# One square instruction per context batch, and one scale per partition

## The reference, cut to what matters

```
x = x + tanh(g_xattn) * ( gelu(layernorm(x) @ ctx.T) @ ctx )      # per batch: 224x512 @ 512x750, 224x750 @ 750x512
x = x + tanh(g_ffn) * moe(layernorm(x))                           # gate, top 2 of 8, silu(x w1) * (x w3), w2
```

## Time and profile before

| | us |
|---|---|
| median of 3 runs | 688.33 (687.57 to 690.29) |
| the profiled execution's own time | 688.32 |
| its span, first to last instruction | 686.6 |
| first GELU of batch 1 to first GELU of batch 14 (13 steps) | 280.93 |
| PE / ACT / DVE / POOL busy, share of the span | 93% / 67% / 61% / 58% |
| mean granted clock of TensorE | 0.991 |

### The profile page before, as it was taken

One profiled execution on the slowest core, in us unless ns is written; L12 is line 12 of the kernel. 1 busy time (PEld: TensorE's weight loads), 2 busy tenths in 40 slices (PEclk: granted clock), 3 DMA queues, 4 the chain that ended last, 5 costly groups with the idle time before them and its releaser, 6 DMA issues.

```text
span 686.6 us, 15832 instructions
## 1 busy us (share of the span) xinstructions
PE 636.1 (93%) x4638; PEld 442.9 (65%) x4639; DVE 416.9 (61%) x1287; ACT 460.6 (67%) x771; POOL 395.6 (58%) x459
## 2 busy tenths in 40 slices
PE   2789999999999999999998999999999999999990
PEld 1677788788887888878885555455554554555550
DVE  3368788898889888898886644543333333333330
ACT  5899999899998999999974444444443444434440
POOL 4332347765666656776566777875555555565551
PEclk9999999999999999999999999999999999999996
DMA  7455558646686567666424565766666656666653
GB/s 216 128 171 157 160 150 200 182 143 181 163 171 195 160 154 189 174 170 179 119 83 120 93 132 93 121 102 120 111 108 121 117 100 122 111 108 118 118 102 55
DMA packets 51380, 94.77 MB, mean 138 GB/s; under 512 B 17024, under 2 KB 25344, under 8 KB 51312
## 3 DMA queue, kind: packets, MB, share of 16 engines
q1 hardware_dynamic: 34096, 60.02, 32.9%
q0 software_dynamic: 16400, 33.89, 27.6%
q10 hardware_dynamic: 816, 0.02, 0.1%
HBM read 61.89 MB, written 32.01 MB: 137 GB/s over the span
## 4 chain that ended last, share of the span: by engine, by line
DMA 26%; PE 11%; issue 5%; DVE 3%; POOL 3%; ACT 1%; POOLq 1%; SPq 0%; DVEq 0%; ACTq 0%
DMA out_rows<-ctx_raw,meta 23%; PE bank L1368 5%; DMA ctx_raw<-xf_rows,meta 3%; PE bank L1377 3%; POOL out_rows L537 2%; PE bank L1323 1%; POOLq L533 1%; PE bank L1357 1%; ACT ctx_raw L766 1%; DMA meta<-route_table 0%; PE bank L1257 0%; PE bank L1222 0%; POOL ctx_raw L525 0%; DVE ctx_part L825 0%; DVE ctxT L1155 0%
## 5 line engine op out<-in xcount | busy, mean ns | idle before, releaser
L1368 PE MATMUL bank<-w,ctxT 128*128 x756 | 173.4, 379 | 0.9 <-issue 0.9
L537 POOL DMA_INDIRECT out_rows<-ctx_raw,meta x63 | 100.3, 1593 | 99.4 <-DMA out_rows<-ctx_raw,meta 87.8
L1222 PE MATMUL bank<-ctx_part,a_part 125*112 125x512 f16 x576 | 135.1, 380 | 0.8 <-DVE a_part L834 0.8
L1368 PEld LDWEIGHTS bank<-w,ctxT 128*128 128x128 f16 x756 | 74.0, 98 | 75.9 <-issue 1.0
L1210 PE MATMUL bank<-xnT,ctxT 128*125 128x224 f16 x1152 | 118.2, 262 | 0.3 <-ACT ctxT L629 0.3
L1210 PEld LDWEIGHTS bank<-xnT,ctxT 128*125 128x125 f16 x1152 | 112.4, 139 | 0.4 <-issue 0.4
L777 ACT ACTIVATE ctxT<-bank,cols 128x256 f32<-128x256 f32 x63 | 29.9, 474 | 115.4 <-issue 84.8
L1222 PEld LDWEIGHTS bank<-ctx_part,a_part 125*112 125x112 f16 x576 | 71.4, 130 | 39.6 <-DVE a_part L834 0.8
L629 ACT ACTIVATE ctxT<-bank 128x1000 f16<-128x1000 f16 x96 | 94.5, 1005 | 3.0 <-PE bank L1177 3.0
L1377 PE MATMUL bank<-w2s,ctxT 128*128 x378 | 91.9, 379 | 1.5 <-DVE ctxT L1137 1.5
L489 POOL DMA_INDIRECT route_table<-route,pos_i x64 | 72.8, 1138 | 19.2 <-issue 17.2
(11 more groups left out here) (155 smaller groups left out, 987.5 us busy)
## 6 DMA issues: line engine op xcount, KB each, us to landing
ctx_raw<-in_ctx SPq DMA_DIRECT2D x48, 448.0 KB
w_raw<-in_L_ffn_w SPq DMA_DIRECT2D x24, 512.0 KB, 6.3
x<-in_x SPq DMA_DIRECT2D x16, 448.0 KB, 6.5
out_rows<-x SPq DMA_DIRECT2D x16, 448.0 KB
xf_rows<-xf SPq DMA_DIRECT2D x16, 448.0 KB, 4.4
ctx_raw<-in_ctx SPq DMA_DIRECT2D x48, 52.0 KB
meta<-route_table SPq DMA_DIRECT2D x66, 1.0 KB, 2.0
ctx_raw<-xf_rows,meta POOLq DMA_INDIRECT x66, 4.2
```

The lines of the kernel that those rows point to most:

```text
L537: g.indirect_dma_start(out=out, out_offset=bass.IndirectOffsetOnAxis(ap=meta[n][:, 0:1], axis=0), in_=y_sb[n % 2], in_offset=None, compute ...
L1222: ins = t_.matmul(O_ps[t][0:TT, :], a_part[ha][:, c, t * TT:(t + 1) * TT], ctx_part[u][hc][:, c, :], start=c == 0 and (ha, hc) == PARTS[0] ...
L1368: ins = t_.matmul(H_ps[u][:, :], rows, w, start=m == 0, stop=m == KD * len(PARTS) - 1)
```

## The change

The sums of squares of a context are now made by one instruction over all three thirds, 125 x 3072, instead of three of 125 x 1024 (`row_squares`, with the instruction at L611 of the new file). It waits for all three loads. Its unwanted output goes to rows 0 to 2 of both the high and the low part of the buffer, which are now two halves of one tensor. There is one sum and one scale for a partition; `scale_from` writes it three times, so that the readers of the scales stay as they are. The high parts of thirds 1 and 2 are made by one instruction of 125 x 2048 (`ctx_high_rest`), in the place where third 1's stood. The maximum over the thirds' totals is left out from batch 2 on. Batches 0 and 1 are begun as before.

```diff
-        ctx_part = [[sb(f"ctx_part{u}{h}", [CR, NC, D], F16) for h in range(2)] for u in range(2)]
+        ctx_both = [sb(f"ctx_part{u}", [CR, 2, NC, D], F16) for u in range(2)]
+        ctx_part = [[b[:, h, :, :] for h in range(2)] for b in ctx_both]
...
+                if copies > 1:
+                    exp = exp.to_broadcast([P, copies])
...
-                scale_from(ctx_sum[:, :], ctx_inv[u][:, :], ctx_s[u][:, :], 0, NQ).then_inc(ctx_scaled, NQ)
+                scale_from(ctx_sum[:, 0:1], ctx_inv[u][:, :], ctx_s[u][:, :], 0, 1, NQ).then_inc(ctx_scaled, NQ)
...
-                seq.done(g.tensor_scalar(ctx_max[:, :], ctx_gsum[:, 0:1], ctx_gsum[:, 1:2], ctx_gsum[:, 2:3], ALU.max, ALU.max))
-                seq.hold()
-                scale_from(ctx_max[:, :], all_inv[:, :], all_s[:, :], A_BITS).then_inc(all_scaled, 1)
+                gmax = ctx_gsum[:, 0:1]
+                if not later(i, 2):
+                    gmax = ctx_max[:, :]
+                    seq.done(g.tensor_scalar(gmax, ctx_gsum[:, 0:1], ctx_gsum[:, 1:2], ctx_gsum[:, 2:3], ALU.max, ALU.max))
+                    seq.hold()
+                scale_from(gmax, all_inv[:, :], all_s[:, :], A_BITS).then_inc(all_scaled, 1)
...
+            def row_squares(i, u):
+
+                for q in range(NQ):
+                    act.wait_ge(ctx_loaded[q], i * 32 + 32)
+                act.wait_ge(ctx_sum_ready, i * NQ)
+                act.wait_ge(ctx_scaled, i * NQ)
+                act.wait_ge(ctx_tot_made, i)
+                act.wait_ge(attn_part, (i - 2) * NQ + 2)
+                a.activation(ctx_both[u][:, :, 0:NC // 2, :], ctx_raw[0:CR, :, :].rearrange("p (h c) d -> p h c d", h=2), ACT.Square,
+                             accum_out=ctx_sum[0:CR, 0:1]).then_inc(ctx_sum_ready, NQ)
...
+            def ctx_high_rest(i, u):
+
+                act.wait_ge(ctx_scaled, i * NQ + NQ)
+                a.activation(ctx_part[u][0][:, 2:NC, :], ctx_raw[0:CR, 2:NC, :], ACT.Copy, scale=ctx_s[u][0:CR, 0:1].bitcast(F32)).then_inc(ctx_high, NQ - 1)
...
                     ctx_high_part(i + 1, w, 0)
-                    ctx_high_part(i + 1, w, 1)
+                    ctx_high_rest(i + 1, w)
                     ctx_tot_out(i + 1)
                     gelu(i, u, 1)
                 split_end(weight_tot_out, i, u, h)
-                ctx_high_part(i + 1, w, 2)
+                if not later(i, 1):
+                    ctx_high_part(1, 1, 2)
...
                 if two:
-                    ctx_squares(i + 2, 0)
-                    ctx_squares(i + 2, 1)
+                    row_squares(i + 2, u)
                 ctxT_out(i + 1, w, 4)
-                if two:
-                    ctx_squares(i + 2, 2)
                 ctxT_out(i + 1, w, 5)
```

More of the change, by code:

```diff
@@ L434, in inv_std, with scale_from @@
                 g.tensor_tensor(rstd[:, at:at + 2], ve[:, at:at + 2], neg_half[:, at:at + 2], ALU.pow).then_inc(out_ready, 1)
-            def scale_from(gmax, inv, s, bits=0, n=1):
+            def scale_from(gmax, inv, s, bits=0, n=1, copies=1):
                 exp, exp_i = exp_f[:, 0, 0:n], exp_f[:, 1, 0:n].bitcast(I32)
```

## The result

| | before | after |
|---|---|---|
| median of the runs, us | 688.46 (6 runs, 686.90 to 690.29) | 708.84 (6 runs, 708.53 to 712.58) |
| ratio to before | | 1.032, 95% interval 1.030 to 1.034 |
| span of the profiled execution | 686.6 | 706.9 |
| mean granted clock of TensorE | 0.991 | 0.977 |

The change makes the kernel 20 us slower. The direction and the mechanism were forecast; the size was not quite: 16.9 us forecast, 20.4 measured. By the ratio the time is 710.2 us on the base that the prediction had (688.33), 0.2 us above the top of its range.

What follows compares the result with a forecast made beforehand. TensorE does nearly all it can, waiting mainly for DVE's `xn`. The change closes a loop through the third load: 13 steps +16.6, neighbours -0.57 and +0.85, together +16.9 on 688.32, so 705.2 us; range 690 to 710.

Steps and rivals of the forecast that it cites:

- closed loop: First GELU, third load's issue, landing, merged square, two copies, next first GELU: 22.08 us short, 23.82 us long steps.
- the sum: Seven short and six long loop steps, 297.5 against 280.93 us; with the neighbouring steps +16.9, so 705.2 us.
- the slip: On ACT, the longer high part starts GELU of third 1 0.85 us later; DVE's run, third load and `xn` follow.
- the 0.57 us of the forecast: On ACT, one square of 3072 in place of three squares saves 0.57 us a step (0.4 to 0.6).
- the loop's terms behind the issue: After the third load's issue: load 6.0 us, merged square 2.74, two copies 1.78.
- The load's time: Third context load, issue to landing: taken as 6.0 us, between bounds of 4.6 and 6.5 us.
- expert stage: Stage after the batch steps: starts later by all of the loss but keeps its length.
- Each microsecond of the load's time is worth 13: Sensitivity of the total to the third load's time, counted once in each of the 13 steps; 6.5 us gives 711.7.
- That rival: Third load lands under some 4.8 us, so the merged square waits little: +2.0, 690.3 us, chance 0.12.
- Queued behind: On ACT, the weight's scale, transposed context and GELU of third 2 slip with DVE's 0.85 us later run.
- over 15 us more idle: Sign of being right: PE waits for `xn` in short steps too, over 15 us more idle in all.

Runs made afterwards that it cites:

- the kernel with filler: The changed kernel plus 22 zero-matrix matmuls a step on PE, from batch 1 on, where it waits: 711.0 us, ratio 1.035.
- the repeated profiles: The kernel before and the changed kernel, each unaltered, profiled once more: 687.2 and 712.9 us.

## Why the prediction came out as it did

**The mechanism was right, with one limit.** The closed loop was forecast part by part, and the profile after has each part. From the first GELU to the issue of the third load: 11.56 and 13.30 us worked out, 290.40 - 278.85 = 11.55 and 268.97 - 255.66 = 13.31 measured. Square 2.75, measured 2.76; high part 1.99, measured 1.99. Steps of 22.08 and 23.82 us were forecast, 22.57 and 23.32 is the mean of those in the loop. The limit: the sum had the loop in all 13 steps, and it holds in 11. The Trainium skill, "ScalarE: Activation LUTs", section "What ACT_TABLE_LOAD costs", gives an ACTIVATE with immediate scale and bias 186 ns and 0.833 ns per element, an estimate of 2745 ns for 3072; the trace's 2762 agrees.

**Load or slip.** In the 13 steps, against 280.93 us before, the slip costs 8.8 us with the three squares left as they were. With the single square and no wait for the third load it costs 1.4; the difference, 7.4, is what the single square saves, 13 times the 0.57 us of the forecast. The wait without the slip costs 8.5 us, with the same saving in it, and the two together 18.5, more than 1.4 and 8.5: once the load is in the loop, the slip delays the load, and the load the next first GELU, so that the slip counts in nearly every step. This was in the sum, and that is why the sum came near.

**The step that failed: the loop's terms behind the issue.** From the landing to the next first GELU I had the square and two copies, 4.52 us, and nothing for ACT's wait instructions. Measured in the short step, it is 301.44 - 296.68 = 4.76: after the landing, the wait instructions take 0.22 us (296.68 to 296.90) before the square starts. In the two steps where the square does not wait for the load, the same instructions pass while the copy ahead of it still runs, and cost nothing. With 4.76 to 4.77 us in each of the 11 steps of the loop this makes 2.7 us. The load's time was one number, 6.0 us, for both kinds of step. It is 6.19 in the short ones, 1.3 us in seven, and 5.25 in the four long ones, -3.0 us. One late issue adds 0.4, and the two steps outside the loop take 0.5 more than forecast. Together 2.7 + 1.3 - 3.0 + 0.4 + 0.5 = 1.9 us, which is 299.40 - 297.5. So the errors cancel in part, and that the 13 steps came within 2 us of the sum is partly luck.

Of the 3.4 us that the profiled execution (708.57 us) has above the forecast of 705.2, these are 1.9. Most of the rest is the expert stage, 1.8 us longer, of which the prediction said that it keeps its length. It took 336.67 us against 334.90; in the repeated profiles the difference is 0.8. How much of it is the change's stays open.

**The clock.** The two steps outside the loop are the term that the prediction did not have at all. Each takes about 0.8 us more than the long steps in the loop (24.08 against 23.32). In PE's timeline of the step from 301.44, whose mean granted clock is 0.93 in its row above, PE sits idle 1.76 and 0.87 us; then four transposes take 1.01 us, against 0.60, and six products 2.21:

```profile
314.45 0.57 PE L1216 MATMUL bank<-ident,xf 112*128 112x112 f32 x4 [1.76 <-ACT xfT L670]
...
316.33 1.01 PE L1216 MATMUL bank<-ident,xn 112*128 112x112 f32 x4 [0.87 <-DVE xn L868]
...
317.97 2.21 PE L1242 MATMUL bank<-ctx_part,a_part 125*112 125x512 f16 x6
```

ACT's wait of 1.38 us at 320.61 follows from it. The steps from 71.91 and 163.41 have a mean of 0.93 too, but there the square still waits for the load, and the parts of the loop are as long as elsewhere. Beside the load, then, the drops are a second and small cause, and without them the load's own time would still set the steps, as the kernel with filler shows.

**The range.** It was drawn from the load's time alone, with every other term as it stood, and ended at 710, while the same text has the forecast reach to 711 and to 712. Seven executions of the changed kernel took 708.5 to 712.9 us. "Each microsecond of the load's time is worth 13" was too much as well: 11 in the first profile, 10 in the second.

**The rivals.** In the 11 steps whose landing the trace shows, the load never landed within 4.8 us: 5.1 was the shortest, and the square waited for it 13.3 us in all. That rival's sum, 690.3 us, came near for the kernel without the wait (692.5, with its long step of 22.61 us measured as 22.62). The Trainium skill, "DMA: Bandwidth & Descriptors", section "Anatomy of one DMA — SWDGE (gpsimd) path", would have given an estimate of 3.2 us; the 5.1 to 7.0 us measured here, for a load that SP issues beside others, do not agree. The section "Rules for kernel authors" of the same page of the Trainium skill advises to wait late on a DMA's semaphore. That agrees, with 16 us between the kernels with and without the early wait.

**Queued behind.** `xn` came late as forecast, and PE waits for it 11 times instead of 7, but only 7.5 us in all against 6.5. The larger new wait is another. That PE would also wait for the transposed `xf`, held on ACT behind the weight whose scale DVE makes late, I named as a slip on ACT, but not as a wait of PE. It is 6.8 us, where it was 0.6 (the last line, of before):

```profile
PE bank L1216 <- DVE xn L868: 7.5, 11, 0.9
PE bank L1216 <- ACT xfT L670: 6.8, 6, 1.8
...
PE bank L1196 <- ACT xfT L648: 0.6, 2, 0.4
```

The prediction's sign of "over 15 us more idle" on PE did not come: its time without work rose by 15.4 - 6.95 = 8.5 us, because its busy time rose too, by 10.0 us for the same matmuls. Part of that is the lower clock in four steps; what the rest is, no run here separates.

## What to carry to other kernels

Merging instructions moves their waits to the earliest place of any part, and their results to the latest. Price both before counting the overhead that is saved: here 0.5 us of ACT's busy time a step (267.15 - 260.61 over 13) was bought with a wait for one load and a slip of 0.85 us, and the two together closed a loop that had been open. Merge what is ready together, and put the merged instruction behind what others wait for. When a load enters a loop, its time counts once per round in which nothing else comes later, with its spread and with the time of the wait instructions behind it.

## What was not expected of the hardware

- Wait instructions have a price when the engine really waits: 0.22 us from the landing to the start of the square, for three of them with rows of their own. Where the instruction ahead of them still runs, they cost nothing.
- The granted clock of TensorE fell to half (from 2.4 to 1.2 GHz) in four long steps of the changed kernel's 13, in two of them within an idle time of 0.9 us that followed one of 1.8; the mean over such a step is 0.93, and in the 13 steps of the kernel before it is 1.00. With filler matmuls in the idle time the mean granted clock of a run rose from between 0.977 and 0.984 to between 0.985 and 0.989.
- The same load of 500 KB took 5.1 to 5.5 us to land in the four long steps and 5.8 to 7.0 in the seven short ones of one execution, and 8.0 us once in the kernel with filler.
